# The last layer's first normalization moved to VectorE alone, and four of its seven output sums to TensorE and ScalarE

## What is computed

```
    h = jnp.maximum(_layernorm(x, axis=-1), 0.0)
    x = x + _L0_gnn_ref(h, adj, ...)      # ends in (Y - mu) / jnp.sqrt(var + LN_EPS) * gamma + beta
    h = jnp.maximum(_layernorm(x, axis=-1), 0.0)
    x = x + _L1_gnn_ref(h, adj, ...)      # einsum('hqm,hmk,hko->qo', att, v, Wo)
```

## Time and profile before

| | us |
|---|---|
| median of three runs | 2347.68 |
| profiled execution | 2348.52 |
| its span, first to last instruction | 2346.7 |
| busy: TensorE, VectorE, ScalarE, GpSimd | 2142.3, 2056.2, 1938.7, 729.3 |
| mean granted TensorE clock | 0.972 of full |

### The profile page before, as it was taken

The page is one execution under the profiler, slowest core; times in us unless marked ns, Lnnn a source line. Parts: engine busy times, 40 slices in busy tenths (PEclk is TensorE's granted clock), DMA queues, the critical chain, the costliest instruction groups (busy, mean ns, idle before and its releaser), DMA issues.

```text
span 2346.7 us, 26070 instructions
## 1 busy us (share of the span) xinstructions
PE 2142.3 (91%) x8250; PEld 1378.1 (59%) x8250; DVE 2056.2 (88%) x3825; ACT 1938.7 (83%) x2849; POOL 729.3 (31%) x987
## 2 busy tenths in 40 slices
PE   7599999999999998998899999999999999999975
PEld 4377677777777676543356555555555555555554
DVE  5699999999999998238869999999999999999995
ACT  5899999999999996257379889889889889889844
POOL 2133443344334433002223232232232332332332
PEclk9699999999999999999999999999999999999987
DMA  7245544554455543332322121221121121122242
GB/s 255 76 111 133 111 98 108 124 111 110 99 123 111 121 94 77 102 98 43 53 53 55 51 45 49 51 57 37 51 58 36 51 58 42 48 56 51 46 117 68
DMA packets 85166, 190.03 MB, mean 81 GB/s; under 512 B 12193, under 2 KB 65056, under 8 KB 85024
## 3 DMA queue, kind: packets, MB, share of 16 engines
q0 software_dynamic: 26208, 61.37, 16.8%
q1 hardware_dynamic: 56496, 125.48, 16.1%
q10 hardware_dynamic: 2320, 1.48, 0.2%
HBM read 154.19 MB, written 34.10 MB: 80 GB/s over the span
## 4 chain that ended last, share of the span: by engine, by line
DVE 48%; PE 24%; ACT 16%; POOL 5%; issue 5%; DMA 0%; SPq 0%; DVEq 0%; ACTq 0%; POOLq 0%
DVE junk L1910 17%; PE bank L1143 11%; ACT junk L1451 6%; DVE logits L2077 6%; DVE small L1954 5%; DVE logits L1946 4%; PE bank L1117 4%; DVE small L1852 3%; POOL small L1736 3%; DVE small L1837 3%; PE bank L1133 2%; ACT logits L1344 2%; PE bank L753 2%; PE bank L1099 2%; PE bank L776 2%
## 5 line engine op out<-in xcount | busy, mean ns | idle before, releaser
L1910 DVE SCALAR_TENSOR_TENSOR junk<-logits,small,expd 128x3327 uint8<-128x3327 f32 x184 | 677.9, 3684 | 4.7
L1143 PE MATMUL bank<-h_aug,turns 128*128 128x256 f32 x2704 | 635.9, 382 | 0.2 <-ACT turns L1473 0.2
L1117 PE MATMUL bank<-both,pair 128*128 128x512 f32 x1352 | 612.3, 597 | 24.3 <-ACT sides L1497 24.2
L1143 PEld LDWEIGHTS bank<-h_aug,turns 128*128 128x128 f32 x2704 | 497.3, 190 | 104.9 <-issue 25.4
L1117 PEld LDWEIGHTS bank<-both,pair 128*128 128x128 f32 x1352 | 251.1, 190 | 309.8 <-issue 261.7
L1117 PE MATMUL bank<-h_aug,both 128*128 128x257 f32 x1352 | 336.7, 398 | 28.0 <-ACT sides L1480 27.7
L1117 PEld LDWEIGHTS bank<-h_aug,both 128*128 128x128 f32 x1352 | 259.1, 198 | 111.0 <-ACT sides L1480 47.3
L1720 POOL TENSOR_TENSOR small<-small 128x1 f32<-128x1 f32 x52 | 14.4, 277 | 881.4 <-DVE small L1979 881.4
L1404 ACT ACTIVATE junk<-expd,small 128x3327 int8<-128x3327 f32 x88 | 270.1, 3069 | 1.5
L1410 ACT ACTIVATE junk<-expd,small 128x3327 int8<-128x3327 f32 x88 | 270.4, 3073 | 0.3
L1133 PE MATMUL bank<-ident,logits 128*128 128x128 f32 x1352 | 193.4, 280 | 61.3 <-DVE logits L2077 51.8
(11 more groups left out here) (250 smaller groups left out, 2972.8 us busy)
## 6 DMA issues: line engine op xcount, KB each, us to landing
both<-adj_turned SPq DMA_DIRECT2D x52, 832.0 KB, 6.6
both<-adj_turned POOLq DMA_DIRECT2D x52, 832.0 KB, 12.0
pair<-adj_turned SPq DMA_DIRECT2D x52, 832.0 KB, 4.5
z<-sides POOLq DMA_DIRECT2D x78, 128.0 KB, 3.2
spread<-sides POOLq DMA_DIRECT2D x26, 128.5 KB, 3.7
turns<-spread SPq DMA_DIRECT2D x26, 128.5 KB, 2.1
attended<-att_out SPq DMA_DIRECT2D x26, 128.0 KB, 1.7
expd<-attended SPq DMA_DIRECT2D x26, 128.0 KB, 2.1
```

The costliest lines, as they stand in the source:

```text
L1117: done = pe.matmul(SX[:, 0:width], half(t, h)[:, bass.ts(jj, P)], rows_of(j), start=(j == 0), stop=(j == T - 1))
L1143: last = pe.matmul(AB[:, 0:D], attT[i % 4][:, b, :], h_aug[:, g + b, 0:D], start=(g + b == 0), stop=(g + b == T - 1))
L1910: chain.did(dve.scalar_tensor_tensor(junk[:, 0:N], logits[t % 3][:, 0:N], col(t, "cand"), expd[t % NE][:, 0:N], ALU.is_gt, ALU.mult, accum ...
```

## The change

VectorE gets a new function `join(g)`: subtract the mean and multiply by gamma (line 2009), then multiply by the reciprocal root and add x (line 2016), one instruction each per tile. With it `scale_own` (ScalarE), `scale_of(0, g)` (VectorE) and `weight_own` (GpSimd) are gone. VectorE measures z one group ahead instead of three. For the groups 0 to 3 (`CARRIED = 4`) TensorE adds x into PSUM by one more product per tile, identity times x (line 1183), and ScalarE copies the sum out (`carry_out`, line 1549) in place of VectorE's `add_own`, which stays for groups 4 to 6.

```diff
                             for i in range(2 * half, 2 * half + 2):
+                                target = OUTS[q % 4][:, bass.ts(i % 2, D)]
                                 for k in range(KT):
-                                    done = pe.matmul(OUTS[q % 4][:, bass.ts(i % 2, D)], hT_of(g)[:, k, bass.ts(i, P)],
-                                                     wvo[:, k, :], start=(k == 0), stop=(k == KT - 1))
+                                    done = pe.matmul(target, hT_of(g)[:, k, bass.ts(i, P)], wvo[:, k, :],
+                                                     start=(k == 0), stop=(k == KT - 1 and g >= CARRIED))
+                                if g < CARRIED:
+                                    done = pe.matmul(target, ident[:, :], x_rows(g)[:, i, :], start=False, stop=True)
...
+                    def carry_out(g):
+                        w = s.GROUPS[g][1]
+                        for half in range((w + 1) // 2):
+                            q = 2 * g + half
+                            act.wait_ge(sem["out_done"], q + 1)
+                            if g >= 2 and half == 0:
+                                act.wait_ge(out_stored[g % 2], g // 2 * 16)
+                            act.activation(out_rows(g)[:, 2 * half:2 * half + 2, :],
+                                           OUTS[q % 4][:, :].rearrange("q (t d) -> q t d", d=D), ACT.Copy
+                                           ).then_inc(sem["out_ready"], 1)
...
-                                scale_own(0)
+                                turned(3, 4)
+                                find_root(1, 0, "var_ready", "root_ready")
                                 find_root(0, 1, "own_var_ready", "own_root_ready")
-                                find_root(0, 2, "own_var_ready", "own_root_ready")
-                                turned(3)
-                                scale_own(1)
-                                turned(4, 5)
-                                scale_own(2)
+                                turned(5)
+                                rectify(0)
                                 turned(6)
-                                for g in range(NG):
-                                    if g + 3 < NG:
-                                        find_root(0, g + 3, "own_var_ready", "own_root_ready")
+                                scale_attended(T - 1)
+                                for g in range(1, NG):
                                     find_root(1, g, "var_ready", "root_ready")
+                                    if g + 1 < NG:
+                                        find_root(0, g + 1, "own_var_ready", "own_root_ready")
                                     rectify(g)
-                                    if g == 0:
-                                        scale_attended(T - 1)
-                                    if g > 0:
-                                        store_last(g - 1)
-                                    if g + 3 < NG:
-                                        scale_own(g + 3)
+                                    store_last(g - 1)
+                                    if 0 < g <= CARRIED:
+                                        carry_out(g - 1)
                                 store_last(NG - 1)
...
                     if not first_step:
-                        for g in range(3):
-                            weight_own(g)
                         add_attended(T - 1)
-                        for g in range(3, NG):
-                            weight_own(g)
...
+                    def join(g):
+                        t, w = s.GROUPS[g]
+                        z, x1 = z_rows(g), x_rows(g)
+                        dve.wait_ge(sem["own_var_ready"], g + 1)
+                        if g == 0:
+                            dve.wait_ge(sem["gamma_loaded"], 16)
+                        for i in range(w):
+                            chain.did(dve.scalar_tensor_tensor(z[:, i, :], z[:, i, :], moments[0][:, t + i, 0:1], gamma_b,
+                                                               ALU.subtract, ALU.mult))
+                        dve.wait_ge(sem["own_root_ready"], g + 1)
+                        chain.did(dve.reciprocal(rstd[0][:, t:t + w], root[0][:, t:t + w]))
+                        dve.wait_ge(sem[f"x_loaded{g}"], 16)
+                        chain.wait()
+                        for i in range(w):
+                            chain.did(dve.scalar_tensor_tensor(x1[:, i, :], z[:, i, :], rstd[0][:, t + i:t + i + 1],
+                                                               x1[:, i, :], ALU.mult, ALU.add))
+                        chain.wait()
...
                     def last_layer():
-                        scale_of(0, 0, "own_root_ready", "own_norm_ready")
-                        for g in range(1, 3):
-                            measure(0, g, "own_var_ready")
-                        dve.wait_ge(sem["found_summed"], 1)
-                        find_flag()
-                        for g in range(1, 3):
-                            scale_of(0, g, "own_root_ready", "own_norm_ready")
                         for g in range(NG):
-                            if g + 3 < NG:
-                                measure(0, g + 3, "own_var_ready")
+                            join(g)
                             measure(1, g, "var_ready")
-                            if g + 3 < NG:
-                                scale_of(0, g + 3, "own_root_ready", "own_norm_ready")
-                            scale_of(1, g, "root_ready", "norm_ready")
-                            if g > 1:
-                                add_own(g - 2)
-                        add_own(NG - 2)
+                            if g + 1 < NG:
+                                measure(0, g + 1, "own_var_ready")
+                            if g == 1:
+                                dve.wait_ge(sem["found_summed"], 1)
+                                find_flag()
+                            scale_of(g)
+                            if g > CARRIED:
+                                add_own(g - 1)
                         add_own(NG - 1)
```

More of the change, by code:

```diff
@@ L29 @@
 LAST_PART = 3
+CARRIED = 4
 PUSH = 0.1
@@ L943, in step @@
                     names += [f"z_loaded{g}" for g in range(NG)] + [f"x_loaded{g}" for g in range(NG)] + [
-                        "gamma_loaded", "own_var_ready", "own_root_ready", "own_norm_ready", "own_scaled", "own_weighted",
-                        "x1_ready", "var_ready", "root_ready", "norm_ready", "h_ready", "hT_done", "hT_stored", "out_done",
+                        "gamma_loaded", "own_var_ready", "own_root_ready", "var_ready", "root_ready", "norm_ready", "h_ready", "hT_done", "hT_stored", "out_done",
                         "out_ready", "found_ready", "found_summed", "flag_ready"]
@@ L988, in step @@
                     rstd = [table(n + 6, 1) for n in range(2)]
-                    shift = [table(n + 8, 1) for n in range(2)]
+                    shift = table(8, 1)
                     eps = QT[:, D + 10 * T * 6:D + 10 * T * 6 + 1]
@@ L1520, in find_root @@
                                        ).then_inc(sem[found_out], 1)
-                    def scale_own(g):
-                        t, w = s.GROUPS[g]
-                        act.wait_ge(sem["own_norm_ready"], g + 1)
-                        for i in range(w):
-                            last = act.activation(z_rows(g)[:, i, :], z_rows(g)[:, i, :], ACT.Identity,
-                                                  bias=shift[0][:, t + i:t + i + 1], scale=rstd[0][:, t + i:t + i + 1])
-                        last.then_inc(sem["own_scaled"], 1)
                     def rectify(g):
@@ L1534, in rectify @@
                             last = act.activation(z_rows(g)[:, i, :], x_rows(g)[:, i, :], ACT.Relu,
-                                                  bias=shift[1][:, t + i:t + i + 1], scale=rstd[1][:, t + i:t + i + 1])
+                                                  bias=shift[:, t + i:t + i + 1], scale=rstd[1][:, t + i:t + i + 1])
                         last.then_inc(sem["h_ready"], 1)
@@ L1812, in gpsimd @@
                             add_columns(t)
-                    def weight_own(g):
-                        w = s.GROUPS[g][1]
-                        pool.wait_ge(sem["own_scaled"], g + 1)
-                        if g == 0:
-                            pool.wait_ge(sem["gamma_loaded"], 16)
-                        pool.tensor_tensor(z_rows(g), z_rows(g), gamma_b.unsqueeze(1).to_broadcast([P, w, D]), ALU.mult
-                                           ).then_inc(sem["own_weighted"], 1)
-                        pool.wait_ge(sem["own_weighted"], g + 1)
-                        pool.wait_ge(sem[f"x_loaded{g}"], 16)
-                        pool.tensor_tensor(x_rows(g), x_rows(g), z_rows(g), ALU.add).then_inc(sem["x1_ready"], 1)
                     if not first_step:
-                        for g in range(3):
-                            weight_own(g)
```

(25 more changed lines are left out.)

## The result

The changed kernel takes 2363.26 us, the median of four runs (2362.78 to 2364.7), against 2347.77 for the kernel before, now of four runs (2346.68 to 2349.67). The ratio is 1.0067, with a 95% interval of 1.0054 to 1.0079: slower by 15.5 us, well above the 0.2% that counts as no change. Forecast were 2362 us and +15.2.

What follows compares the result with a forecast made beforehand. It took ScalarE's chain and VectorE's line 2022, waiting for GpSimd, as the bound. Terms -9.0 + 6.1 + 6.1 = +3.2, plus 12 for TensorE's clock, +15.2 us: 2362 us, range 2349.5 to 2366.5.

Steps and rivals of the forecast that it cites:

- The mechanism: Groups 2 to 5: the root waits behind `carry_out`'s copies, so one group's loop takes 9.7 us against VectorE's 7.5.
- Start of the last layer: Group 1's `rectify` and norm: VectorE goes straight into `join(0)`, so group 1 comes 9.0 us earlier.
- Periods at full clock: Group 1's `rectify` to group 5's: four periods of 9.7 us, 38.8 against 32.66, a loss of 6.1 us.
- Tail at full clock: After group 5's `rectify`: `add_own(4)` ahead of `join(6)` makes 19.2 us of 13.15, a loss of 6.1 us.
- The clock: TensorE's six bursts in the last layer: gaps lose the full clock, 2.0 us for each, 12 us in all.
- the forecast's two rows: Earlier TensorE bursts that lost the clock: at least 1.5 us for a low stretch within, 2.5 if low from the start.
- B with one fall: Rival on TensorE's clock: it stays up, 2350.9 us, or with one fall about 2353; chance 0.17 for none or one.
- VectorE: VectorE's work per group after the change: multiply-adds 0.40 us apart, 7.5 us in all (6.6 to 8.2).
- the dearer row: A TensorE burst low from its start, 2.5 us lost; six such bursts would make 15 us.
- Rival A: Groups 1 to 5: the wait for `carry_out` doesn't bind, VectorE's 7.5 us sets the period, 2342 us; chance 0.07.

Runs made afterwards that it cites:

- a1: The changed kernel with ScalarE's copies of `carry_out` moved behind the next group's `rectify`: 2344.7 us.
- b1: The kernel before with line 2022's shift written as one single-column instruction with a scalar operand per row tile: 2335.0 us.
- d3: The kernel before with the shift in single columns and unread products in three of TensorE's gaps: 2332.5 us.
- a3: The changed kernel with unread products added to fill TensorE's gaps, nothing else changed: 2351.1 us.
- a2: The changed kernel with VectorE's `add_own(4)` moved behind group 6's `join` and `scale_of`: 2354.7 us.
- c1: The changed kernel with both edits, copies behind the next `rectify` and `add_own(4)` behind group 6's scale: 2336.3 us.
- d1: c1 with `store_last(g - 1)` placed ahead of `carry_out(g - 2)` on ScalarE: 2333.7 us.

## Why the prediction was right

- *The mechanism.* "`scale_of(g + 1)` waits for that root", which stands behind the copies: shown by the chain of the changed kernel, and by a1, where moving the copies takes the wait away.
- *Start of the last layer:* forecast 9.0 us earlier for group 1's `rectify`, measured 26.97 - 16.85 = 10.1 (from the end of the selection step). The wait for `turned(4)` was 0.7 us shorter than summed: TensorE's transposes began at 2271.98 for 2272.72. This fits its clock, which had come back 1.5 us earlier than in the trace before (2267.1 for 2268.7). I put that down to luck and not to the change: in b1 and d3, which lack the change, it also came back 2.1 to 2.6 us after the selection step, against 2.2 in the changed kernel and 3.8 in the trace before. `find_flag` took 0.64 us for 0.8.
- *Periods at full clock:* forecast 9.7 us, 9.80 in a3; four of them 39.2 against 32.7 before, 6.5 us lost for 6.1. In the changed kernel, with its falls, they were 11.3, 12.6, 11.3 and 12.6.
- *Tail at full clock:* forecast 19.2 us, 75.70 - 56.21 = 19.5 in a3; lost 6.3 for 6.1. a2 shows that it is the order of `add_own(4)` and `join(6)`.
- *The clock:* forecast 12 us (six bursts at 2.0), measured 12.3 (changed kernel less a3). The gap of 3.4 us was summed rightly (3.39). That it would lose the clock was a weighing of rows that pointed both ways, with 0.66 for a loss in most bursts. Each fall cost 2.05 us on average, but not evenly: a burst of transposes and 24 records took 7.95 us when the low stretch lasted 3.4 us, and 9.2 us when it lasted 6.8, against 6.4 at full clock in a3. So the low stretches cost 1.5 and 2.8 us, near the forecast's two rows (1.5 and 2.5), and they came in turn. Taking the middle was right for the sum of six and for none of them alone; that the sum came so close is luck in part.
- One reading of the trace before was loose: after the "4.1 us idle" the clock was still up, but a burst of 1.1 us (2284.68) followed, and the clock fell at 2285.7, within it. So a gap of 4.2 us (2280.46 to 2284.68) had lost the clock, and that row spoke for a fall more plainly than the prediction said. And B with one fall (2352.9) was counted as "same", though it lies just above the prediction's own bound of 2352.4.
- *VectorE:* multiply-adds 0.40 apart as in the earlier trace rows; 7.26 us per group (a1) for the 7.5 forecast.
- The Trainium skill's rule on the clock (TensorE: Matmul & The Clock Gate, HAM oscillation) would have made it 15 us with the dearer row; its direction, a loss on every pass, held in six of six bursts here and in four of five in a2. Rival A (the port decides, 2342) describes a1 (2344.7), not the change: VectorE did get its time back, and the new wait took more than that.

With the start as it was in a3 (10.0 us earlier) the terms add up: -10.0 + 6.5 + 6.3 + 12.3 = +15.1 us, of 15.2 measured in the profiles. The forecast's terms were -9.0 + 6.1 + 6.1 + 12. Its start was 1 us short of the gain and the other three were 1 us short of the losses, so part of the agreement is errors that cancel.

## What to carry to other kernels

A copy that waits for another engine's long burst must not stand in a queue ahead of a tiny instruction on which the next stage depends: here a root of 0.3 us behind two copies made the difference between 2363 and 2345 us, with the same work. Before an engine is emptied to free a port, see which instruction waits for the port and whether it can be written with one input; one rewritten instruction did about as much as the best form of the whole rearrangement. Products that fill TensorE's gaps pay only where its bursts are waited for; measure the layer with and without them, since a clock at 1.00 by itself is no gain.

## What the runs showed of the hardware

- Gaps of 3.4 to 5.6 us lost the clock in six of six bursts of the changed kernel (3.72, four times 3.39, 5.55). In a2 one burst behind a gap of 3.39 us kept it and three lost it. The length alone doesn't decide below that either: 2.70 us kept it in the kernel before, while 1.92 us in b1 and 2.06 us in d3 lost it. Gaps under 1 us kept it in a1, c1 and d1.
- The low stretches in the changed kernel lasted some 3.4 us and some 6.8 us in turn, and so its periods alternate between 11.3 and 12.6 us. The long ones are those that began within the gap.
- VectorE's instructions on one column with a scalar operand took 0.58 us for four while GpSimd's product ran (b1), where one instruction with two inputs in SBUF took up to 2.31 us (before).
